# A state-space layer: statistics of two normalisations moved to ScalarE, and a fifth of sixteen state products moved to GpSimd

## What is computed

```
x = layernorm(x + linear_attention(x, W))
x = layernorm(x + moe_32_experts_top4(x))
x = layernorm(x + state_space(x))          # the change is here
x = layernorm(x + moe_8_experts_top2(x))
layernorm(x) = (x - mean) / sqrt(var + 1e-5)   # over the 128 columns
state_space(x):  x, z = split(x @ in_proj.T); x = silu(conv4(x) + b)
                 dt = softplus(x @ w_dt ...); B, C = x @ w_bc  (16 states each)
                 h[n,t] = exp(dt[t] * A[n]) * h[n,t-1] + dt[t] * x[t] * B[n,t]
                 y[t]   = sum over n of h[n,t] * C[n,t]  + x[t] * D
                 out    = (y * silu(z)) @ out_proj.T
```

## Time and profile before

| | us |
|---|---|
| median of three runs (1744.99, 1745.33, 1748.7) | 1745.33 |
| the profiled execution: whole | 1742.75 |
| its span from first to last instruction | 1741.0 |
| busy: PE / DVE / POOL / ACT | 1393.9 / 1352.9 / 1367.5 / 972.2 |

### The profile page before, as it was taken

How to read it: one execution, slowest core, us unless ns; L and a number is a source line. 1 busy time by engine, 2 the same in 40 slices (tenths; PEclk the granted TensorE clock), 3 DMA queues, 4 the chain that set the end, 5 groups by cost and what they waited for, 6 DMA issues and landing times.

```text
span 1741.0 us, 23137 instructions
## 1 busy us (share of the span) xinstructions
PE 1393.9 (80%) x5849; PEld 832.6 (48%) x5890; DVE 1352.9 (78%) x2623; ACT 972.2 (56%) x1681; POOL 1367.5 (79%) x949
## 2 busy tenths in 40 slices
PE   5778744426998899889988998898897797999990
PEld 3666643312443344334433443343343476998970
DVE  3888831112999999999999999999999858657777
ACT  2665511104655665566556646655664465887873
POOL 2656566753999999999989989999999477777575
PEclk8999955557999999999989999999899999999995
DMA  5433243325382422342234123312521323555544
GB/s 149 127 101 121 84 89 59 43 40 187 117 254 115 141 84 73 123 140 73 80 127 140 62 86 132 133 56 90 178 80 55 118 69 97 165 155 155 147 107 135
DMA packets 195131, 195.44 MB, mean 112 GB/s; under 512 B 22520, under 2 KB 174008, under 8 KB 190776
## 3 DMA queue, kind: packets, MB, share of 16 engines
q1 hardware_dynamic: 172280, 168.95, 30.0%
q0 software_dynamic: 22784, 25.71, 7.3%
HBM read 137.26 MB, written 59.80 MB: 113 GB/s over the span
## 4 chain that ended last, share of the span: by engine, by line
PE 42%; DVE 26%; issue 15%; POOL 9%; ACT 2%; DMA 2%; DVEq 1%; SPq 1%; POOLq 0%; another core or an unknown queue 0%; ACTq 0%
PE bank L1340 13%; DVE hst L1757 12%; PE bank L1295 6%; PE bank L1433 2%; DVE prod L1779 2%; PE bank L1446 2%; POOL dbx L825 2%; PE bank L1430 2%; PE bank L1457 2%; PE bank L1456 2%; POOL yg L892 2%; PE bank L1329 1%; PE bank L1353 1%; PE bank L1293 1%; POOL xe L759 1%
## 5 line engine op out<-in xcount | busy, mean ns | idle before, releaser
L825 POOL TENSOR_TENSOR dbx<-u,ball 128x1024 f32<-128x1024 f32 x256 | 613.8, 2497 | 5.3 <-POOL u L862 2.8
L1757 DVE TENSOR_TENSOR_SCAN hst<-bank,dbx 128x512 f32<-128x512 f32 x512 | 592.0, 1205 | 11.2 <-POOL dbx L825 6.7
L1340 PE MATMUL bank<-prod,ident 128*128 128x512 f32 x1024 | 514.0, 639 | 23.4 <-DVE prod L1779 18.0
L1029 ACT ACTIVATE bank<-dt,aneg 128x511 f32<-128x511 f32 x512 | 346.4, 688 | 278.8 <-DVE hst L1757 276.8
L1340 PEld LDWEIGHTS bank<-prod,ident 128*128 128x128 f32 x1024 | 207.4, 205 | 263.6 <-issue 209.9
L1779 DVE TENSOR_TENSOR prod<-hst,bank 128x1024 f32<-128x1024 f32 x192 | 233.4, 1216 | 17.2 <-DVE hst L1757 13.8
L834 POOL TENSOR_TENSOR prod<-hst,call 128x1024 f32<-128x1024 f32 x64 | 161.0, 2515 | 22.9 <-DVE hst L1757 22.8
L892 POOL DMA_INDIRECT yg<-expert_rows,row_of x128 | 124.5, 972 | 50.7 <-issue 38.5
L1324 PE MATMUL bank<-parts,sel_c 128*128 128x512 bf16 x152 | 61.1, 403 | 73.8 <-DVE prod L1779 73.1
L1295 PE MATMUL bank<-x2T,inc 128*128 128x512 f32 x256 | 116.5, 598 | 0.0
L880 POOL DMA_INDIRECT sorted_rows<-x3b,row_of x80 | 79.3, 991 | 27.9 <-issue 25.3
(11 more groups left out here) (294 smaller groups left out, 2765.4 us busy)
## 6 DMA issues: line engine op xcount, KB each, us to landing
ball<-b_rows SPq DMA_DIRECT2D x32, 2048.0 KB, 7.1
call<-b_rows SPq DMA_DIRECT2D x16, 1024.0 KB, 9.5
xr<-sorted_rows SPq DMA_DIRECT2D x44, 256.0 KB
expert_rows<-yu SPq DMA_DIRECT2D x44, 256.0 KB, 2.7
sorted_rows<-blank SPq DMA_DIRECT2D x2, 4096.0 KB
xg_rows<-xg SPq DMA_DIRECT2D x16, 320.0 KB, 2.5
xt<-in_x SPq DMA_DIRECT2D x16, 256.0 KB, 2.9
xT<-in_xT SPq DMA_DIRECT2D x16, 256.0 KB, 3.1
```

What stands on the lines that cost most here:

```text
L825: gp.tensor_tensor(dbx[n % NDB][:, :, :], u[s.par][:, :, :], ball[:, n:n + 1, :].to_broadcast([P, NH, SEQ]), ALU.mult).then_inc(dbx_rdy, 1)
L1029: act.activation(da_ps[h][:, 1:SEQ], dt_[s.par][:, h, 1:SEQ], ACT.Exp, scale=aneg[:, h, n:n + 1]).then_inc(da_rdy, 1)
L1340: last = mm(y_ps[:, h, :], ident[:, :], from_[:, h, :], start=False, stop=(n == NS - 1), skip_group_check=True)
L1757: dve.tensor_tensor_scan(h_of[:, h, :], da_ps[h][:, :], dbx[n % NDB][:, h, :], 0.0, ALU.mult, ALU.add).then_inc(scan_rdy, 1)
```

## The change

The state list of POOL gets a fifth member, 13, and so DVE makes 11 products instead of 12. Since 11 is odd, the choice among two buffers now goes by `turn(s, n)`, which counts on over sequences. Both statistics leave DVE: ACT makes them as sums along the row (an Identity with `accum_out` gives -mean/sqrt(128), a Square with that as bias gives the variance), four and four instructions for each normalisation. POOL keeps the two instructions for 1/sqrt(var+eps); the product with the mean goes to DVE as one small instruction (`shift_of`). Places: sums of `m` at ACT's step 2 and squares at step 4, POOL's scale at step 5 (was 4), DVE's shift at step 6, ACT's application at step 6 (was 5); sums of `ahead` at ACT's steps 12 and 13, squares at 14, POOL's scale at step 15 as before, DVE's shift at step 0 of the next iteration, behind `gated`. The main parts of the diff:

```diff
-ON_POOL = (1, 4, 7, 10)
+ON_POOL = (1, 4, 7, 10, 13)
...
+def turn(s, n):
+    return (s.off * ND + place(n)) % 2
...
-            def scale_shift(r, n, m, s, ready, done, last):
+            def scale_of(r, var, s, ready, done, last):
                 gp.wait_ge(ready, s.at(8, 8))
                 need(gp, last, s.at(TT))
                 settle(gp)
-                gp.tensor_scalar(r[:, :], m[:, :, 1], LN_EPS, None, ALU.add).then_inc(done, 1)
-                gp.wait_ge(done, s.at(4, 1))
+                gp.tensor_scalar(r[:, :], var[:, :], LN_EPS, None, ALU.add).then_inc(done, 1)
+                gp.wait_ge(done, s.at(3, 1))
                 gp.tensor_tensor(r[:, :], r[:, :], neghalf[:, 0:TT], ALU.pow).then_inc(done, 1)
-                gp.wait_ge(done, s.at(4, 2))
-                settle(gp)
-                gp.tensor_tensor(n[:, :], m[:, :, 0], r[:, :], ALU.mult).then_inc(done, 1)
-                gp.wait_ge(done, s.at(4, 3))
-                settle(gp)
-                gp.tensor_scalar(n[:, :], n[:, :], -1.0, None, ALU.mult).then_inc(done, 1)
...
-                    if m and n == 4:
-                        scale_shift(rs2, nm2, mv2, m, m_mv, m_rs, x3_rdy)
+                    if m and n == 5:
+                        scale_of(rs2, var2, m, m_mv, m_rs, x3_rdy)
...
+            def sums(src, spill, shift, tiles, done):
+                for k in tiles:
+                    act.activation(spill[:, k, :], src[:, k, :], ACT.Identity, scale=-1.0 / (D * ROOT_D), accum_out=shift[:, k:k + 1]
+                                   ).then_inc(done, 1)
+
+            def squares(src, spill, shift, var, s, done):
+                act.wait_ge(done, s.at(8, 4))
+                for k in range(TT):
+                    act.activation(spill[:, k, :], src[:, k, :], ACT.Square, bias=shift[:, k:k + 1], scale=1.0 / ROOT_D,
+                                   accum_out=var[:, k:k + 1]).then_inc(done, 1)
...
-                    if m and n == 5:
-                        act.wait_ge(m_rs, m.at(4, 4))
+                    if m and n == 2:
+                        act.wait_ge(op_mm, m.at(1, 1))
+                        need(act, m_rs, m.at(3))
+                        need(act, st_x3[m.par], m.half(16))
+                        sums(blk4(pc_ps), x3o[m.par], shift2, range(TT), m_mv)
+                    if m and n == 4:
+                        squares(blk4(pc_ps), x3o[m.par], shift2, var2, m, m_mv)
+                    if ahead and n == 12:
+                        act.wait_ge(ld_s[ahead.par], ahead.half(16, 16))
+                        need(act, f_rs, ahead.at(3))
+                        sums(rin[ahead.par], spill, shift1, range(0, 2), f_mv)
+                    if ahead and n == 13:
+                        sums(rin[ahead.par], spill, shift1, range(2, TT), f_mv)
+                    if ahead and n == 14:
+                        squares(rin[ahead.par], spill, shift1, var1, ahead, f_mv)
+                    if m and n == 6:
+                        act.wait_ge(m_rs, m.at(3, 3))
...
-            def stats_ahead(s):
-                dve.wait_ge(ld_s[s.par], s.half(16, 16))
-                need(dve, f_rs, s.at(4))
-                stats_of(rin[s.par], st1, mv1, s, f_mv)
+            def shift_of(n, shift, r, s, done):
+                dve.wait_ge(done, s.at(3, 2))
+                stt(n[:, :], shift[:, :], ROOT_D, r[:, :], ALU.mult, ALU.mult).then_inc(done, 1)
...
-                    if m and n == 3:
-                        dve.wait_ge(op_mm, m.at(1, 1))
-                        need(dve, m_rs, m.at(4))
-                        stats_of(blk4(pc_ps), st2, mv2, m, m_mv)
+                    if m and n == 6:
+                        shift_of(nm2, shift2, rs2, m, m_rs)
+                    if f and n == 0:
+                        shift_of(nm1, shift1, rs1, f, f_rs)
                     if f:
                         front(f, n)
-                    if ahead and n == NS - 2:
-                        stats_ahead(ahead)
```

More of the change, by code:

```diff
@@ L41 @@
 LN_EPS = 1e-5
+ROOT_D = 128 ** 0.5
 BATCH = (6, 6, 4)
@@ L315, in build @@
             x3o = [mb(f"x3o{p}", [P, TT, D]) for p in range(2)]
-            st1 = mb("st1", [P, TT, 6])
-            mv1 = mb("mv1", [P, TT, 2])
+            spill = mb("spill", [P, TT, D])
+            shift1 = mb("shift1", [P, TT])
+            var1 = mb("var1", [P, TT])
             rs1 = mb("rs1", [P, TT])
             nm1 = mb("nm1", [P, TT])
-            st2 = mb("st2", [P, TT, 6])
-            mv2 = mb("mv2", [P, TT, 2])
+            shift2 = mb("shift2", [P, TT])
+            var2 = mb("var2", [P, TT])
             rs2 = mb("rs2", [P, TT])
@@ L840, in iteration @@
                         gp.wait_ge(scan_rdy, NB * NS * NH)
+                        gp.wait_ge(pprod_rdy, NB * NP)
                         for k in range(2):
@@ L865, in iteration @@
                     if ahead and n == NS - 1:
-                        scale_shift(rs1, nm1, mv1, ahead, f_mv, f_rs, x2_rdy)
+                        scale_of(rs1, var1, ahead, f_mv, f_rs, x2_rdy)
             gp.wait_ge(added, E0 // 2 * 16)
@@ L870, in _ @@
             load_second(Seq(0, 0))
-            scale_shift(rs1, nm1, mv1, Seq(0, 0), f_mv, f_rs, x2_rdy)
+            scale_of(rs1, var1, Seq(0, 0), f_mv, f_rs, x2_rdy)
             schedule(gp, iteration)
@@ L978, in front @@
                 if n == 0:
-                    act.wait_ge(f_rs, s.at(4, 4))
+                    act.wait_ge(f_rs, s.at(3, 3))
                     need(act, res_mm, s.at(1, -1))
@@ L1075, in _ @@
             act.wait_ge(m_init, 1)
+            act.wait_ge(ld_s[0], 16)
+            sums(rin[0], spill, shift1, range(TT), f_mv)
+            squares(rin[0], spill, shift1, var1, Seq(0, 0), f_mv)
             schedule(act, iteration)
@@ L1323, in spread_c @@
                 need(pe, prod_rdy, s.at(ND, k - 1))
-                mm(cb_ps[k % 2][:, :], sel_c[:, n, :], parts[s.par][:, :], start=True, stop=True).then_inc(cb_rdy, 1)
+                mm(cb_ps[turn(s, n)][:, :], sel_c[:, n, :], parts[s.par][:, :], start=True, stop=True).then_inc(cb_rdy, 1)
             def skip_term(s):
@@ L1337, in add_state @@
                     pe.wait_ge(prod_rdy, s.at(ND, k + 1))
-                    from_, done = prod[k % 2], y_mm
+                    from_, done = prod[turn(s, n)], y_mm
                 for h in range(NH):
@@ L1747, in iteration @@
                     k = place(n)
-                    h_of = hst[2 if n in ON_POOL else k % 2]
                     if s:
+                        h_of = hst[2 if n in ON_POOL else turn(s, n)]
                         dve.wait_ge(dbx_rdy, s.at(NS, n + 1))
@@ L1778, in iteration @@
                         need(dve, y_mm, s.at(ND, k - 1))
-                        tt(prod[k % 2][:, :, :], h_of[:, :, :], over_h(cb_ps[k % 2]), ALU.mult).then_inc(prod_rdy, 1)
+                        tt(prod[turn(s, n)][:, :, :], h_of[:, :, :], over_h(cb_ps[turn(s, n)]), ALU.mult).then_inc(prod_rdy, 1)
             dve.wait_ge(added, E0 // 2 * 16)
@@ L1793, in _ @@
             dve.wait_ge(m_init, 1)
-            stats_ahead(Seq(0, 0))
             schedule(dve, iteration)
```

## The result

The changed kernel takes 1767.44 us (median of four runs, 1764.61 to 1768.39) against 1745.99 (four runs): a ratio of 1.0118, interval 1.01 to 1.0135. It is slower by 21 us where 10 us of gain were forecast, and outside the range of 1724 to 1759. The profiled execution's span is 1765.2 us against 1741.0.

A forecast was written before the change was run, and what follows sets the result against it. DVE and POOL were taken as full, PE close behind, at 58.7 us per sequence. A 58.0 period gave -0.7 x 15 = -10.5, with head and tail +0.8: -9.7, so 1735.5 us on the median, range 1724 to 1759.

The forecast's parts named there:

- the cost of the shift: On DVE, two added 128x4 shifts per sequence, taken at 0.2 us each.
- The loop, forecast 58.0: Gate period per sequence: 57.6 where PE's clock holds, 58.4 with a long slow spell before the gate, half and half.
- Rival A: POOL alone sets the pace at 57.5 per sequence and PE is never late: 1728 us, chance 0.20.
- the statistics' removal: On DVE, statistics of `ahead` shorten the loop by 1.32; those of `m`, 1.13, mostly become a wait for PE.
- POOL rises to be the highest sum: With the fifth product POOL's floor goes up by 0.8 to 57.5 us per sequence, highest of all.
- PE at the gate: PE idles 1.7 to 2.2 before product 14; the gate waits 0 at full clock, 1.5 or 2.5 with slow spells.
- sixteen activations with an accumulated output: On ACT, 0.45 us each, 7.2 per sequence, raising ACT from 66% to 80% of its time.
- Rivals B and D: B: ACT is the new wait, no change, 1745 us, 0.17. D: such as extra table loads, 1776 us, 0.04.
- Scan 14: On DVE, it waits about 0.5 us for ACT, whose two sums at step 12 delay decay 14.
- The transfer of five rows: On SP, the `call` waits for POOL's product 13, 2.3 later; hidden unless it takes over 15.9 us.
- Head +1.8 and tail -1: Head gains 1.8 us from sums and squares before the first scale; tail loses 1 in DVE's routing chain.
- Rival C: PE's slow spell moves behind the gate, slowing skip term, transposes and convolutions: 59.9 per sequence, 1764 us, chance 0.19.

The follow-up runs named there:

- e1: The changed kernel with both shifts made on ScalarE (four 128x1 Identity activations each) instead of VectorE: 1730.12 us, ratio 0.99.
- e11: The changed kernel with four states on GpSimd instead of five, shifts still on VectorE: 1731.02 us, ratio 0.9893.
- e3: The kernel before plus a needless 128x4 scalar_tensor_tensor from two SBUF tensors on VectorE at steps 0 and 6: 1772.3 us, ratio 1.0152.
- e9: The kernel before plus six needless two-SBUF-tensor instructions on VectorE per sequence, of differing kind, place and width: 1791.16 us, one run.
- e4: The kernel before plus a needless 128x4 tensor_scalar from one SBUF tensor on VectorE at steps 0 and 6: 1775.58 us, ratio 1.0156.
- e2: The changed kernel with each shift still on VectorE but as four 128x1 tensor_scalar instructions with a scalar pointer: 1728.43 us, ratio 0.9884.
- e6: e1 with four states on GpSimd instead of five: 1719.82 us, ratio 0.9843.
- e7: The kernel before with only the fifth state moved to GpSimd and buffers chosen by turn(s, n): 1755.21 us, ratio 1.0041.
- e12: The changed kernel with the shift made on GpSimd, as a small instruction behind its pow: 1733.68 us, ratio 0.9916.
- e10: The changed kernel with the step 6 shift on ScalarE and the step 0 shift still on VectorE: 1761.11 us, ratio 1.0067.
- e5: The kernel before plus eight needless VectorE instructions of different forms per sequence, each at its own step: 1866.81 us, one run.

## Why the prediction was wrong

The step that failed is the cost of the shift: "It gains two shifts of 128x4. No row shows one on DVE; POOL's like it takes 0.20, DVE's whole product 1.22: I take 0.2, being the same tiny shape." It measured 2.0 in the mean, and 2.31 at most gates. Shape was the wrong thing to go by: the nearest rows were POOL's own, and DVE's product, which reads one operand from PSUM. The scans, products and gates of DVE's loop all read PSUM with one SBUF tensor, and none of them stood. The statistics of `rin` read SBUF alone and did not stand either: in the earlier trace rows four of them took 0.86, beginning at 1067.90 beside this POOL instruction of the kernel before:

```profile
1066.14 2.35 POOL L862 TENSOR_TENSOR u<-dt,xc 128x1024 f32<-128x1024 f32 x1 [0.24 <-POOL dt L857]
```

So the loop of before held no instruction of the standing forms, and its trace gave no warning. The loop grew to 60.2 per sequence, against 57.7 in e1, which has the same work without the stall: 2.5 x 15 = 37 us of the 42.3 between the two spans. Against the forecast 58.0 it is 2.2, or 33 us; that 1735.5 + 33 comes to just the measured time is partly chance, since e1 itself came out 5 us under the forecast. Besides the cost, a second step was missed: the forecast took the fifth state and the shift for independent terms, and e11 shows that they are not.

The Trainium skill has the rule: GPSIMD Engine Reference, section 8, Key points, says that GpSimd shares its SBUF interfaces with VectorE, and that VectorE's instructions contend in a two-port mode or with two SBUF inputs. The runs agree where there are two tensors: medians of 1.75 us in e3, 1.85 and 1.87 in e9. They agree with the other half if the tensor_scalar of four elements (median 1.9, e4) ran in such a mode and that of one element (0.2, e2) did not; no run here shows the mode itself. The shift is the one instruction of the change of this kind, and the prediction did not weigh the rule.

The rest, step by step:

- The loop, forecast 58.0: right in size, in part by luck. With the stall taken out the mean period is 57.7 and the time 1730 to 1728, against 1735.5. But 58.0 was the mean of 57.6 and of 58.4 in sequences with a slow spell of PE before the gate, and in e1 nearly all periods are 58.0 to 58.1, with no wait for PE at any gate but the last. Rival A had that part right (PE never late), with 57.5 a little too short.
- That the statistics' removal shortens the loop by 1.32 where they stood ahead of product 14 and by little in PE's half: right. e6 stands at 56.94.
- POOL rises to be the highest sum with a fifth state: borne out by e7 and by POOL's 98% in e1, while e12 shows that it isn't the only bound. It means that the fifth state was a loss in itself, 10 us between e6 and e1. The prediction's own terms give 56.7 for the DVE and PE loop with four states (58.35 - 1.32 - 0.3, worked out for e6) against 57.5 with five, but it did not draw that out.
- PE at the gate: its mechanism wrong, its price small. PE stood idle 4.22 before product 14, not 1.7 to 2.2, and the twelve matmuls took 7.01; yet the gate hardly waited (0.2 to 0.36 at four gates, 1.42 at the last, nothing at the others), since DVE waited 2.37 for dbx 0, which the prediction had listed as a sign. POOL's long wait before its first product, which was to vanish, was 1.25 in the changed kernel and is gone in e1.
- ACT: sixteen activations with an accumulated output run at 0.25 to 0.39 from start to start, the read of the accumulator (0.2) mostly hidden; 0.45 had been taken. No table load was added: 39 in the whole kernel, as before. POOL didn't wait for the squares but at head and tail. Rivals B and D fall with that. Scan 14 came 0.23 late (a piece of four scans took 4.79 against 4.56), not 0.5:

```profile
1044.58 0.26 ACT L1027 ACTIVATE x3o<-bank 128x128 f32<-128x128 f32 x1
1044.74 0.19 ACT L1027 ACTIVATION_READ_ACCUMULATOR x3o<-bank 128x1 f32 x1
1044.83 0.27 ACT L1027 ACTIVATE x3o<-bank 128x128 f32<-128x128 f32 x1
```

- The transfer of five rows landed in 8.3 us (median), within the 15.9 allowed.
- Head +1.8 and tail -1: not borne out. The first gate came 1.8 later, but in the experiments with the same eight activations ahead of it it stood anywhere from 484.66 (e1) to 491.48 (e10), against 487.20 before. From the last gate to the end it is 373.3 us in the changed kernel and 373.2 before.
- Rival C named nearly the measured time, 1764, by a wrong cause. PE does run dry before and behind y2 (1.39 and 1.44), but its skip term took 1.98 at its gate, as it did before (1.99), and the clock over the stage was no lower (0.96 against 0.94).

## What to carry to other kernels

Before a small VectorE instruction is priced by its shape, ask where its operands lie and what GpSimd does meanwhile: with two SBUF tensors, or as a copy or tensor_scalar of two or four float32, it took as long as GpSimd's running instruction had left, here up to 2.3 us and at one place (e5) 7.9. If it also waits for GpSimd's result, or is released by the same event, it starts just behind GpSimd's next one and pays nearly the whole of it. Give it a form that didn't stand here (tensor_scalar of one column at a time, e2) or another engine (e1). And don't move work to the engine whose sum is already nearly the longest: here that cost 10 us by itself, and it tied the stall to the worst moment.

## What was not expected of the hardware

- A tensor_scalar of 128x4 from one SBUF tensor stands like one with two (e4, 1.9 us), of 128x1 it does not (0.12 and 0.2).
- One two-tensor instruction let four GpSimd instructions pass, 7.9 us, in 13 of 16 sequences (e5); others got in at the first boundary, also between two dbx without a gap.
- A transfer issued by GpSimd did not hold a shift up: 0.16 us at 390.31, inside the issue of `rin`.
- The read of ScalarE's accumulator is an instruction of its own of 0.2 us; the next activation starts 0.09 us after it does (1044.74, 1044.83).
